# An eight-layer transformer kernel: its setup products reordered, and the last pair's L1X row sums moved to TensorE

## The reference, cut to what matters

```
x = x + L0X(norm(x), ctx);  x = x + L0F(norm(x))   # L0F: 8 heads of self-attention, 8 experts for values and outputs, best two by gate
x = x + L1X(norm(x), ctx);  x = x + L1F(norm(x))   # L1X: 16 heads of 8 columns, causal and length masks
x = x + L2X(norm(x), ctx);  x = x + L2F(norm(x))   # L1F: weights rounded to -1, 0, 1 by their mean absolute value
x = x + L3X(norm(x), ctx);  x = x + L3F(norm(x))   # L3X: 16 heads of 64 columns

def L1X(x, ctx):
    q, k, v = x @ WQ + bQ, ctx @ WK + bK, ctx @ WV + bV      # split in 16 heads
    p = softmax(q @ k.T / sqrt(8) + causal, masked by lengths)
    return (p @ v) @ WO + bO
```

## Time and profile before

| | before |
|---|---|
| median of 3 runs | 651.56 us (649.15 to 652.43) |
| profiled execution | 650.43 us, span 648.8 |
| PE busy | 629.2 us, 5582 records |
| DVE, ACT, POOL busy | 504.2, 367.1, 212.4 us |
| HBM | 110 MB read, queues 49.7% busy |

### The profile page before, as it was taken

How to read it: one execution, slowest core, us unless ns; L and a number is a source line. 1 busy time by engine, 2 the same in 40 slices (tenths; PEclk the granted TensorE clock), 3 DMA queues, 4 the chain that set the end, 5 groups by cost and what they waited for, 6 DMA issues and landing times.

```text
span 648.8 us, 14778 instructions
## 1 busy us (share of the span) xinstructions
PE 629.2 (97%) x5582; PEld 580.7 (90%) x5582; DVE 504.2 (78%) x1352; ACT 367.1 (57%) x1255; POOL 212.4 (33%) x252
## 2 busy tenths in 40 slices
PE   8999999899999999999999999999999999898889
PEld 7899999788999999999889999988899999567878
DVE  3886677898696868887987889879778586775776
ACT  3442132377465747354665677568666563866774
POOL 1000004465031512424531444154343531643040
DMA  8986969887614734899525318451552720000000
GB/s 339 413 285 217 308 215 330 295 281 255 238 38 131 260 123 134 293 302 349 169 90 175 103 47 289 162 193 35 162 202 98 268 74 5 6 2 1 2 2 9
DMA packets 37078, 111.93 MB, mean 173 GB/s; under 512 B 8976, under 2 KB 11664, under 8 KB 36496
## 3 DMA queue, kind: packets, MB, share of 16 engines
q1 hardware_dynamic: 37008, 110.99, 49.7%
HBM read 109.93 MB, written 1.05 MB: 171 GB/s over the span
## 4 chain that ended last, share of the span: by engine, by line
PE 88%; ACT 5%; DVE 4%; DMA 2%; issue 1%; POOL 0%; SPq 0%; DVEq 0%; ACTq 0%
PE bank L489 37%; PE e_bank L489 37%; PE p_bank L489 5%; PE bank L785 4%; ACT wide_b L1190 3%; DMA gated<-gates_of 2%; PE bank L774 1%; DVE gated L1499 1%; PE p_bank L594 1%; ACT wide_a L1045 1%; PE e_bank L688 1%; PE bank L1023 1%; PE bank L867 1%; DVE f_route L1499 0%; PE bank L627 0%
## 5 line engine op out<-in xcount | busy, mean ns | idle before, releaser
L489 PE MATMUL e_bank<-weights,gated 128*128 128x128 f32 x1984 | 235.2, 275 | 0.7 <-DVE gated L1499 0.7
L489 PEld LDWEIGHTS e_bank<-weights,gated 128*128 128x128 f32 x1984 | 228.2, 192 | 3.9 <-issue 1.6
L1190 ACT ACTIVATE wide_b<-wide_b,max_neg 128x120 f32<-128x120 f32 x272 | 103.4, 385 | 10.0 <-DVE max_neg L1805 6.2
L1397 POOL TENSOR_TENSOR wide_b<-wide_b,row_inv 128x480 f32<-128x480 f32 x64 | 70.9, 1114 | 115.1 <-DVE row_inv L1816 115.0
L1499 DVE TENSOR_TENSOR gated<-gated,f_v 128x1024 f32<-128x1024 f32 x64 | 77.2, 1234 | 9.1 <-DMA gated<-gates_of 5.0
L1389 POOL TENSOR_TENSOR rstd<-var_eps,w_const 128x1 f32<-128x1 f32 (+1 forms) x48 | 33.7, 702 | 152.9 <-DVE var_eps L1495 152.8
L1499 DVE TENSOR_TENSOR gated<-gated,f_xnT 128x1024 f32<-128x1024 f32 x60 | 77.8, 1333 | 2.8 <-DMA gated<-gates_of 2.6
L1045 ACT ACTIVATE wide_a<-bank 120x512 f32<-120x512 f32 (+5 forms) x103 | 53.5, 539 | 46.1 <-PE bank L489 19.0
L1190 ACT ACTIVATION_READ_ACCUMULATOR wide_b<-wide_b,max_neg 128x1 f32 x272 | 52.1, 191 | 0.0
L1805 DVE TENSOR_REDUCE max_neg<-wide_b 128x4 f32<-128x480 f32 x64 | 41.8, 653 | 2.2
L1045 ACT ACTIVATE f_v<-e_bank 128x512 f32<-128x512 f32 x32 | 19.2, 600 | 36.1 <-PE e_bank L489 36.1
(11 more groups left out here) (274 smaller groups left out, 1236.8 us busy)
## 6 DMA issues: line engine op xcount, KB each, us to landing
gated<-gates_of SPq DMA_DIRECT2D x124, 512.0 KB, 5.6
weights<-in_experts SPq DMA_DIRECT2D x64, 512.0 KB, 6.1
w_L2f<-in_L2f SPq DMA_DIRECT2D x1, 2124.0 KB, 16.8
w_L3x<-in_L3x SPq DMA_DIRECT2D x1, 2108.0 KB, 11.9
w_L3f<-in_L3f SPq DMA_DIRECT2D x1, 1128.0 KB, 14.1
wide_b<-in_raw0f SPq DMA_DIRECT2D x1, 1024.0 KB, 7.5
w_L1f<-in_L1f SPq DMA_DIRECT2D x1, 516.0 KB, 8.0
x_next<-in_x SPq DMA_DIRECT2D x4, 128.0 KB, 4.6
```

Source lines behind the costliest of these rows:

```text
L489: return nc.tensor.matmul(o, lhsT, rhs, start=first, stop=last)
L1190: last = nc.scalar.activation(p, p, ACT.Exp, bias=max_neg[lane][:, h:h + 1], accum_out=row_sum[lane][:, h:h + 1])
L1397: nc.gpsimd.tensor_tensor(p3, p3, row_inv[lane][:, 4 * i:4 * i + 4].unsqueeze(2).broadcast_to([128, 4, K]), ALU.mult).then_inc(probs_norme ...
```

## The change

- **Zeros:** 7 products before the fold become 5, `WARM` goes from 14 to 6; `front_steps` waits for the filled zeros too.
- **Loads:** L3X's pack now has `wq` first. Its 1024 columns are loaded ahead of L3F, the other 3192 behind the first four expert weights, ahead of the masks. `pair_mask` counts on `lens_loaded`.
- **Setup order:** on TensorE after L2X's values: L2X's `wq` (Q2_TURNED), L3X's `wq` in two steps, `up`, `gate`/`fc1`, `w1`/`w2`, Q2, and only then PROJ_BIAS, PROJ_TOTAL and L1F's `fc`. ScalarE's copies follow that. VectorE's threshold becomes a step of its own, and the ternary step is split in two. The scratch of `q2_turned` and `centred_fc1` moves to `wide_a[0]`.
- **Last pair, L1X:** ScalarE's exponentials make no row sum; GpSimd doesn't multiply; TensorE turns the plain exponentials, and makes the row sums with 16 more products of 32 columns (ones in `head_cols`) into columns S to 2S of the mix's bank; VectorE inverts those and multiplies the mix by them, in place of ScalarE's copy. The products go strip by strip. `MOVED` becomes 1 for L1X, stays 2 for L3X.
- **A new `ORDER`** for all engines.

```diff
-MOVED = 2
-WARM = 14
+MOVED_L1X, MOVED_L3X = 1, 2
+WARM = 6
...
-                    for pack in ("L2x", "L3x", "L3f"):
-                        sp.dma_start(part[pack][:, :], packs[pack]).then_inc(loaded[pack], 16)
+                    sp.dma_start(part["L2x"][:, :], packs["L2x"]).then_inc(loaded["L2x"], 16)
+                    sp.dma_start(part["L3x", "wq"], packs["L3x"][:, 0:1024]).then_inc(l3_queries_loaded, 16)
+                    sp.dma_start(part["L3f"][:, :], packs["L3f"]).then_inc(loaded["L3f"], 16)
                     for j in range(W_SLOTS):
                         load_weights(j)
+                    rest = width(PACKS["L3x"])
+                    sp.dma_start(part["L3x"][:, 1024:rest], packs["L3x"][:, 1024:rest]).then_inc(loaded["L3x"], 16)
...
-                    keep_busy(7)
+                    keep_busy(5)
...
-                    pe.wait_ge(loaded["L3x"], 16)
+                    pe.wait_ge(l3_queries_loaded, 16)
                     for half in range(2):
-                        pe.wait_ge(centred, FC + half)
+                        if half == 0:
+                            pe.wait_ge(setup_computed, ABS_TAKEN)
+                        else:
+                            pe.wait_ge(centred, Q2_TURNED)
                         mm(bank[0][half][:, :], centre, part["L3x", "wq"][:, 512 * half:512 * half + 512])\
                             .then_inc(centre_products, 1)
-                    yield
+                        yield
...
                     pe.wait_ge(blocks_ready[lane], blocks_ready.upto(L1X, 3, pair))
                     wait_turned(pe, lane, L1X, 1, pair)
-                    wait_turned(pe, lane, L1X, 3, pair)
-                    for c in range(4):
+                    if pair == PAIRS - 1:
                         for j in range(4):
-                            h = 4 * j + c
-                            last = mm(bank[lane][2][32 * j:32 * j + 32, 0:S], v[lane][0:K, 32 * h:32 * h + 32],
-                                      wide_a[lane][0:K, 128 * h:128 * h + 128], c == 0, c == 3)
+                            if j >= 2:
+                                wait_turned(pe, lane, L1X, j, pair)
+                            r = slice(32 * j, 32 * j + 32)
+                            for c in range(4):
+                                h = 4 * j + c
+                                mm(bank[lane][2][r, S:2 * S], part["const", "head_cols"][0:K, 32 * c:32 * c + 32],
+                                   wide_a[lane][0:K, 128 * h:128 * h + 128], c == 0, c == 3)
+                            for c in range(4):
+                                h = 4 * j + c
+                                last = mm(bank[lane][2][r, 0:S], v[lane][0:K, 32 * h:32 * h + 32],
+                                          wide_a[lane][0:K, 128 * h:128 * h + 128], c == 0, c == 3)
+                            if j < 3:
+                                yield
...
-                            last = nc.scalar.activation(p, p, ACT.Exp, bias=max_neg[lane][:, h:h + 1],
-                                                        accum_out=row_sum[lane][:, h:h + 1])
+                            if layer == L1X and pair == PAIRS - 1:
+                                last = nc.scalar.activation(p, p, ACT.Exp, bias=max_neg[lane][:, h:h + 1])
...
+                        if late_sums:
+                            dve.wait_ge(mix_psum[lane], mix_psum.upto(L1X, 1, pair))
+                            link(nc.vector.reciprocal(wide_b[lane][:, S:2 * S], bank[lane][2][:, S:2 * S]))
+                            tt(wide_b[lane][:, 0:S], bank[lane][2][:, 0:S], wide_b[lane][:, S:2 * S], ALU.mult)\
+                                .then_inc(mixT_ready[lane], 1)
+                            yield
```

More of the change, by code:

```diff
@@ L903, in back_lane @@
                     yield
-                    wait_turned(pe, lane, L2X, MOVED if pair == PAIRS - 1 else 0, pair)
+                    wait_turned(pe, lane, L2X, 0, pair)
                     for h in range(H2X):
@@ L1176, in late_setup @@
                     yield
+                    act.wait_ge(setup_products, PROJ_BIAS)
+                    copy(proj_rows[:, :], bank[0][0][:, 0:D]).then_inc(setup_taken, 1)
+                    yield
+                    act.wait_ge(setup_products, PROJ_TOTAL)
+                    copy(proj_scratch[:, 0:D], bank[0][1][:, 0:D], scale=-1.0 / 512).then_inc(setup_taken, 1)
+                    yield
+                    act.wait_ge(centre_products, FC)
+                    copy(part["L1f", "fc"], bank[0][0][:, :]).then_inc(centred, 1)
+                    yield
                 def back_lane(pair, lane):
@@ L1204, in softmax_banks @@
                                 yield
-                            if n >= behind and (pair < PAIRS - 1 or n - behind >= MOVED):
+                            if n >= behind and n - behind >= moved(layer, pair):
                                 take_transposed(layer, n - behind, lane)
@@ L1218, in back_lane @@
                     yield from softmax_banks(L1X, 2)
[L1219 to L1221 removed]
+                    if pair < PAIRS - 1:
+                        act.wait_ge(mix_psum[lane], mix_psum.upto(L1X, 1, pair))
+                        copy(wide_b[lane][:, 0:S], bank[lane][2][:, 0:S]).then_inc(mixT_ready[lane], 1)
+                        yield
                     act.wait_ge(kv_psum[lane], kv_psum.upto(L2X, 1, pair))
@@ L1393, in normalise_probs @@
                     def normalise_probs(layer):
+                        if layer == L1X and pair == PAIRS - 1:
+                            return
                         for i in range(4):
-                            pool.wait_ge(inv_ready[lane], inv_ready.upto(layer, i + 1, pair))
+                            pool.wait_ge(inv_ready[lane], normed_upto(inv_ready, layer, i + 1, pair))
                             p3 = wide_b[lane][:, 4 * K * i:4 * K * (i + 1)].rearrange("p (h k) -> p h k", k=K)
@@ L1823, in softmax_banks @@
                             yield
-                        invert_sums(layer, 0, lane)
-                        yield
+                        late_sums = layer == L1X and pair == PAIRS - 1
+                        if not late_sums:
+                            invert_sums(layer, 0, lane)
+                            yield
                         take_scores(layer, 3, lane, scale, added)
```

160 lines of the change are left out of this document (88 added, 72 removed).

## The result

| | before | changed |
|---|---|---|
| median (5 runs each) | 651.56 us (649.15 to 653.44) | 657.99 us (657.13 to 659.43) |
| ratio, 95% interval | 1 | 1.0102 (1.0084 to 1.0119) |
| profiled execution | 650.43 us, span 648.8 | 657.34 us, span 655.3 |

The account below looks back on a forecast made before the run. TensorE's own work bounds 130 to 545 us, latency the tail; 650.43 - 4.3 (start) + 9.5 (tail) = 655.6 for the profiled execution, 656.8 on the median, forecast 656.5. Its own range is 652 to 661, with rivals 645 to 663.

Parts of the forecast that it names:

- The start, minus 4.3: Setup up to the full stretch: fewer zeros and centring moved up start the expert products earlier, 4.3 us saved.
- fewer zeros: Very start of TensorE's queue: the fold begins about 0.8 us earlier, 0.5 of that carried to the first pair.
- the prediction's own walk: New table with old durations: fifth expert product at 45.6 against 50.39, ninth at 57.3 against 61.06.
- sum of 5.0 for the centring: Setup products of L2X, L3X's queries and L3F moved up: 5.0 us out of the full part of TensorE's queue.
- Rival (b): Start gives nothing back, since gated tiles are the bound from 60 to 130 us: 660.5 us; chance 0.10.
- The tail, plus 9.5: Last pair's L1X: lane 0's x 10.0 us later, 0.5 given back behind it.
- The strips: Last pair's L1X sums and mixes on TensorE: 64 records a lane taken at 7.0 us, bounds 1.8 and 7.1.
- ScalarE's 3.9 us: Last pair's L1X: 32 exponentials without accumulated sum, 0.26 us each instead of 0.383, save 3.9 us.
- The reciprocal of 128 columns, 0.95 by slope: VectorE, last pair's L1X: 0.95 us from reciprocals of 32 and 16 elements; 1.25 with the multiply.
- Rival (a), strips overlap: Last pair's L1X: a lane's products take 1.8 us, total 646.8 us, faster; chance 0.18.
- Rival (c), half taken up: Tail: the lanes untangle and 4 of the 9.5 us return, total 652 us; chance 0.18.
- Rival (d), the clock: Fewer zeros: TensorE's clock rises later or falls waiting for gates, 10 us more, 666 us; chance 0.03.

Follow-up runs that it names:

- zeros_back: Changed kernel with 35 products of zeros as before instead of 17; one profiled execution: span 656.5 us, fifth expert product at 47.39.
- strips_apart: Changed kernel with the strip in the inner loop, so neighbouring sums and mixes write different 32-partition strips; 651.34 us, 0.9992 to the kernel before.
- slots_3_7: Changed kernel with seven slots for gated tiles and three for expert weights instead of six and four; 680.45 us, 1.0455 to the kernel before.
- lane1_sums: Changed kernel with the strip innermost and the last pair's row sums by TensorE in lane 1 alone; 650.31 us, 0.9991 to the kernel before.
- tile_later: Changed kernel with pair 0's gated tile 25 behind pair 1's second maximum and four best-two steps on VectorE; 658.11 us, 1.0118 to the kernel before.
- new_start_old_tail: Changed kernel with gated tile 25 later and the last pair's L1X as before, its first steps in the changed order; 650.76 us, 0.9993 to before.
- start_only: Changed kernel without its changes to the last pair's L1X (tail tables of the kernel before); 650.15 us, 0.9976 to the kernel before.

## Why the prediction was right

Forecast 656.5, measured 657.99. By its steps:

- **The start, minus 4.3.** Right where it was worked out: fifth product 45.99 (predicted 45.6), ninth 57.39 (57.3), first full tile 43.98 (44.1), best-two 20.77 (20.3), half tiles 28.82 (28.2). Not all for the reason given: fewer zeros were credited with 0.5, for those ahead of the fold; in `zeros_back` it is the later ones that lie on the path, with 1.1. Wrong in carrying the 4.3 to the end: 2.2 reach the first take. The 4.3 also doesn't follow from the prediction's own walk, which gives 4.8 at the fifth product and 3.8 at the ninth; 0.2 more than that is 4.0, and the measured 3.7 at the ninth is close. (Its sum of 5.0 for the centring adds up to 5.1, and nothing hangs on it.) Rival (b) had the mechanism, gates that can't come sooner, but put it at nothing given back; half is. Gates account for 1.8 of the loss (4.8 at the 17th product, 3.0 at pair 1's first), and waits in the new order for the other 0.8, which no rival had. What spoke for rival (b) was the 85% of the engines in the earlier trace rows. What I set against it, that TensorE waits only 3.7 us in that stretch, told how things stood at the old pace, not how much room was left.
- **The tail, plus 9.5.** It is 8.7, with two errors of opposite sign: 10.0 at lane 0's x is 8.5, and behind it 0.2 are added where 0.5 were to be given back. Times after the first take, in us:

| | before | predicted | measured |
|---|---|---|---|
| lane 1's mix starts | 11.7 | 8.0 | 8.1 |
| lane 1's x | 14.0 | 17.6 | 16.5 |
| lane 1's gelu | 17.2 | 21.0 | 20.0 |
| lane 0's x | 22.7 | 32.7 | 31.2 |

  The strips were mis-sized: 7.0 us a lane, measured 5.9, since at each border between strips a few records overlap. That is 1.1 in each lane.
- **ScalarE's 3.9 us.** It is 2.6: the 32 exponentials are busy 9.5 us, not 8.2. The earlier trace rows is a row of gelus that read PSUM; the exponentials start 0.29 apart, not 0.26:

```profile
L1229 ACT ACTIVATE wide_b<-wide_b,max_neg 128x120 f32<-128x120 f32 x32 | 9.5, 388 | 1.2 <-DVE max_neg L1852 1.2
```

- **The reciprocal of 128 columns, 0.95 by slope.** Measured 0.96; with the multiply 1.25.
- **The sum.** 650.43 - 2.2 + 8.7 = 656.9 against 657.34 for the profiled execution. The start was taken 2.1 too good, the tail 0.8 too bad. That the forecast missed by only 1.5 is in part luck, since these two have opposite signs.
- **Rival (a), strips overlap.** Its price for the strips was right, 1.8 us, and `strips_apart` shows it with 1.9, but only for the other order of the loops. Its price for the whole was too low even then: 0.5 us off the old tail, where `strips_apart` adds 1.3. The Trainium skill, "TensorEngine Tiling (Array Packing)", Key Properties, says that different tiles can run in parallel; the trace agrees to the letter, for tiles that are different and next to one another. Its section Theoretical Speedup gives up to 4x for a side of 32; here it is 3.8 (0.112 against 1.89/64, 0.030), and 1 for neighbours on the same strip.
- **Rival (c), half taken up:** no; behind lane 0's x the tail is 0.2 longer, not shorter.
- **Rival (d), the clock.** It didn't decide, but it is there, at another place; see below.

## What to carry to other kernels

Before narrow products are moved, added or split, look at which neighbours in the queue write the same strip: order them with the strip innermost. Work taken out ahead of a stretch that is fed by DMAs moves its due times forward as well; read how far the feeding can follow (issue to landing, and what is idle in between) before the gain is carried to the end. And in a hand-made order, one tile with late data holds everything behind it on its engine, so the wait shows under another engine's name.

## What the runs showed of the hardware that I had not expected

**The clock falls after the wait, in some executions.** In `strips_apart`, whose start is that of the changed kernel, TensorE waits the same 2.77 us to 100.15. Granted clock behind it, in `strips_apart` and in the changed kernel:

```profile
102.00:107.00 5.00, 5.00 (x29) 5.00 (x28) 4.37 (x5) 1.73 (x9) 0.00 (x0) 0.58 0.66 254
```
```profile
102.00:107.00 5.00, 5.00 (x47) 5.00 (x46) 5.00 (x5) 1.60 (x9) 0.00 (x0) 1.00 1.03 330
```

29 records in 5 us instead of 47, most of them at the lower of the clock's two levels; pair 1's first product is then at 127.22 instead of 124.20. It is a matter of the execution: of 73 executions of kernels with the new start (`slots_3_7` not counted) 43 have a mean granted clock under 1.00, all 12 of `lane1_sums` among them; of the 72 of the kernel before 9. It doesn't take the long wait: `tile_later`, with no wait over 0.7 us from 90 to 124 us, has it in 4 of 6, and in its trace the fall (0.72 from 118 to 124 us) comes behind five waits of 0.4 to 0.7. Nor does the mean say where it falls: of the six traces of these kernels that have it, it is between 95 and 130 us in five and in the first 20 us in two (`lane1_sums` and `new_start_old_tail`), where the clock is 0.91. In `start_only`, 6 of 12 have it, with a median of 650.7 us against 649.3 for the others: about 1.4 us. So a wait of 2 to 3 us in a full stretch can cost as much again, and the profiled execution of the changed kernel was one without. The Trainium skill, "TensorE: Matmul & The Clock Gate", section What's actually happening, has the granted clock go by how busy TensorE has been; the direction agrees, and that the same wait lowers it in one execution and not in the next is only in these runs. What decides it stays open.

**The clock rises early in the run, but not at the same place in each execution.** TensorE's first rows, of the changed kernel, of `lane1_sums` (the same instructions up to here) and of `zeros_back`:

```profile
1.04 3.35 PE L503 MATMUL e_bank<-small 128*128 128x128 f32 x14 [1.04 <-DVE small L1564]
4.18 1.97 PE L503 MATMUL bank<-wide_a 128*128 128x128 f32 x8
```
```profile
1.04 3.30 PE L507 MATMUL e_bank<-small 128*128 128x128 f32 x14 [1.04 <-DVE small L1567]
4.26 1.16 PE L507 MATMUL bank<-wide_a 128*128 128x128 f32 x8
```
```profile
1.04 4.58 PE L503 MATMUL e_bank<-small 128*128 128x128 f32 x24 [1.04 <-DVE small L1564]
5.45 1.06 PE L503 MATMUL bank<-wide_a 128*128 128x128 f32 x8
```

Ahead of the fold stand 14, 14 and 24 records of zeros. In the changed kernel the fold's own eight records start 0.21 apart, the pace of the zeros, and the pace goes to 0.11 only at about 6.2 us. In `lane1_sums` it does so at 4.5, in `zeros_back` at 4.5 too, in the kernel before at 5.7. So against `zeros_back` the fold starts 1.27 us earlier in the changed kernel and ends 0.4 earlier, and in `lane1_sums` it starts 1.2 and ends 1.1 earlier. What sets the place isn't shown. Where the rise falls late, the slow records are those of real products. None of this reached the path here: the next thing that TensorE waits for is the first normed x, at 9.19 us in the changed kernel. (The column of the granted clock shows 1.00 here in all of them; the pace of the records shows the level.)

**The start scatters.** With the same instructions the fifth expert product starts between 45.63 and 47.56. The late one, `lane1_sums`, can be taken apart: its constants land at 8.2 us instead of 7.6, and TensorE turns the first normed x 0.6 later. It has waited 1.97 us for it, where the changed kernel waited 0.64, and behind that wait the granted clock is 0.50 from 12 to 14 us, where the changed kernel's is 1.00: 1.0 us more. That is the fall of the clock after a wait once again. The full stretch hardly scatters: from pair 1's first to the last expert product it takes 416.9 us in seven of the kernels (first and last: 124.20 and 541.07 in the changed one).
